# Moving the early samples' sum and its dots behind the last group's matmuls in TensorE's program of a three-layer CIN kernel

## The reference

```python
for (W, b), split in zip(conv_params, split_flags):        # 3 layers
    z = jnp.einsum('bhd,bmd->bhmd', x, x0).reshape(B, h * x0.shape[1], D)
    xk = jax.nn.relu(jnp.einsum('oc,bcd->bod', W, z) + b[None, :, None])
    if split:
        x, xk = (xk[:, :half], xk[:, half:])
    results.append(xk)
pooled = jnp.sum(jnp.concatenate(results, axis=1), axis=2)  # [512, 256]
return pooled @ Wo.T + bo                                   # [512, 1]
```

## Time and profile before

| | before |
|---|---|
| median of 3 runs | 482.07 us (482.01 to 482.96) |
| the profiled execution | 480.3 us |
| its span, first to last instruction | 478.5 us |
| PE busy | 443.9 us (93%) |
| DVE busy | 424.8 us (89%) |
| POOL busy | 408.4 us (85%) |
| ACT busy | 310.7 us (65%) |
| TensorE clock granted, mean | 0.982 |

### The profile page before, as it was taken

One profiled execution on the slowest core, in us unless ns is written; L12 is line 12 of the kernel. 1 busy time (PEld: TensorE's weight loads), 2 busy tenths in 40 slices (PEclk: granted clock), 3 DMA queues, 4 the chain that ended last, 5 costly groups with the idle time before them and its releaser, 6 DMA issues.

```text
span 478.5 us, 5975 instructions
## 1 busy us (share of the span) xinstructions
PE 443.9 (93%) x1601; PEld 302.7 (63%) x1601; DVE 424.8 (89%) x489; ACT 310.7 (65%) x383; POOL 408.4 (85%) x147
## 2 busy tenths in 40 slices
PE   0758599999999999999999999999999999999994
PEld 0325276766667676666767676666767676677672
DVE  1556599999999999999999999999999999999994
ACT  1224667686858677676858677676857677686650
POOL 0107499998999999999999999999999999999991
PEclk9998599999999999999999999999999999999999
DMA  8999999989695959689695959689594954630100
GB/s 210 244 232 223 256 226 209 210 191 205 137 227 120 219 126 221 136 186 209 136 231 112 223 124 222 136 191 204 136 232 112 222 122 98 133 79 10 44 0 1
DMA packets 23232, 78.42 MB, mean 164 GB/s; under 512 B 5939, under 2 KB 5939, under 8 KB 18996
## 3 DMA queue, kind: packets, MB, share of 16 engines
q1 hardware_dynamic: 23220, 78.28, 74.5%
HBM read 61.48 MB, written 0.00 MB: 128 GB/s over the span
## 4 chain that ended last, share of the span: by engine, by line
PE 81%; DMA 6%; DVE 5%; issue 2%; ACT 2%; SPq 2%; POOL 1%; DVEq 0%
PE y_ps L706 25%; PE y_ps L694 14%; PE y_ps L712 14%; PE y_ps L696 14%; PE y_ps L702 7%; DVE z L534 4%; PE y_ps L718 3%; DMA a_rep<-x_sb 3%; DMA w_raw<-w_dram 2%; DMA shifted<-xt_dram 1%; ACT zh L423 1%; PE y_ps L672 1%; POOL zl L481 1%; SPq L329 1%; PE y_ps L698 1%
## 5 line engine op out<-in xcount | busy, mean ns | idle before, releaser
L481 POOL TENSOR_TENSOR zl<-z,zh 128x1024 fp32r<-128x1024 f32 (+1 forms) x141 | 406.6, 2919 | 48.6 <-ACT zh L423 48.2
L534 DVE TENSOR_TENSOR z<-a_ps,b_fac 128x1536 f32<-128x1536 f32 x254 | 269.6, 1083 | 25.7 <-PE y_ps L718 13.2
L423 ACT ACTIVATE zh<-z 128x1024 fp32r<-128x1024 f32 (+1 forms) x141 | 176.8, 1254 | 113.2 <-DVE z L534 112.9
L712 PE MATMUL y_ps<-zl,w_high 128*128 128x512 f32 x332 | 154.6, 559 | 1.9 <-POOL zl L481 1.9
L694 PE MATMUL y_ps<-zh,w_high 128*128 128x512 f32 x332 | 131.9, 397 | 10.1 <-ACT zh L423 10.1
L696 PE MATMUL y_ps<-zh,w_low 128*128 128x512 f32 x332 | 130.8, 394 | 0.0
L706 PE MATMUL y_ps<-z,w_raw 128*128 128x512 f32 x254 | 129.5, 591 | 0.0
L712 PEld LDWEIGHTS y_ps<-zl,w_high 128*128 128x128 f32 x332 | 62.4, 189 | 70.1 <-issue 61.8
L694 PEld LDWEIGHTS y_ps<-zh,w_high 128*128 128x128 f32 x332 | 62.8, 189 | 25.4 <-issue 6.4
L696 PEld LDWEIGHTS y_ps<-zh,w_low 128*128 128x128 f32 x332 | 63.0, 190 | 13.8
L706 PEld LDWEIGHTS y_ps<-z,w_raw 128*128 128x128 f32 x254 | 47.9, 189 | 10.6
(11 more groups left out here) (45 smaller groups left out, 164.8 us busy)
## 6 DMA issues: line engine op xcount, KB each, us to landing
b_fac<-xt_dram SPq DMA_DIRECT2D x60, 512.0 KB, 9.0
shifted<-xt_dram SPq DMA_DIRECT2D x64, 256.0 KB, 4.9
a_rep<-x_sb SPq DMA_DIRECT2D x96, 128.0 KB, 3.0
shifted<-xt_dram SPq DMA_DIRECT2D x64, 128.0 KB, 5.2
a_rep<-x_sb SPq DMA_DIRECT2D x64, 64.0 KB, 2.7
b_fac<-xt_dram SPq DMA_DIRECT2D x8, 256.0 KB, 10.7
w_raw<-w_dram SPq DMA_DIRECT2D x2, 640.0 KB, 13.1
w_raw<-w_dram SPq DMA_DIRECT2D x2, 384.0 KB, 12.5
```

The source lines that it names most:

```text
L423: nc.scalar.activation(zh[:, slot, 0:end - native, :], z[:, slot, native:end, :], ACT.Copy).then_inc(zh_ready, 1)
L481: nc.gpsimd.tensor_tensor(zl[:, slot, 0:end - native, :], z[:, slot, native:end, :], zh[:, slot, 0:end - native, :].bitcast(F32), ALU.subtract
L534: return nc.vector.tensor_tensor(dst, factor.unsqueeze(1).to_broadcast(list(dst.shape)), others, ALU.mult)
L712: mm = nc.tensor.matmul(y, wh[layer][:, w, :], zl[:, slot, t, :], start=False, stop=end_here)
```

## The change

On PE, the sum of the early samples (line 645) and the dots of layers 1 and 2, with their waits, leave the place ahead of the last group and stand behind that group; the order among them becomes dot of layer 1, the sum, dot of layer 2, then as before the dot of layer 3 behind its wait for the last pooling. On DVE, the bias addition over 480 samples leaves the end of `early_samples` and stands behind the last pooling, ahead of the addition for the last 32 samples. No instruction is added, removed or resized.

```diff
@@ early_samples (DVE)
-                dve.wait_ge(out_summed, 1)
-                dve.wait_ge(bo_loaded, 16)
-                nc.vector.tensor_scalar(out_sb[:, 0:EARLY], y_ps[1][0:1, 0:EARLY], bo_sb[0:1, 0:1], None, ALU.add
-                                        ).then_inc(out_ready, 1)
@@ DVE, end of the program
             iterate(dve, body, NCHUNK + 2)
+            dve.wait_ge(out_summed, 1)
+            dve.wait_ge(bo_loaded, 16)
+            nc.vector.tensor_scalar(out_sb[:, 0:EARLY], y_ps[1][0:1, 0:EARLY], bo_sb[0:1, 0:1], None, ALU.add
+                                    ).then_inc(out_ready, 1)
             dve.wait_ge(out_summed, 2)
@@ PE, body
-                    if i_is(i, NCHUNK + 1) and g == GROUPS[3] - 1:
-
-                        pe.wait_ge(ones_set, 1)
-                        pe.wait_ge(terms_made, 3)
-                        nc.tensor.matmul(y_ps[1][0:1, 0:EARLY], ones[:], terms[:], start=True, stop=True
-                                         ).then_inc(out_summed, 1)
-
-                        pe.wait_ge(pooled12_done, NCHUNK + 1)
-                        pe.wait_ge(results_ready[3], NCHUNK - 1)
-                        dot(3, RESULTS[1], pooled12, EARLY, start=True).then_inc(last_begun, 1)
-                        pe.wait_ge(last_begun, 1)
-                        dot(3, RESULTS[2], pooled12, EARLY + SAMPLES)
@@ PE, end of the program
             iterate(pe, body, NCHUNK + 1)
 
+            pe.wait_ge(pooled12_done, NCHUNK + 1)
+            pe.wait_ge(results_ready[3], NCHUNK - 1)
+            dot(3, RESULTS[1], pooled12, EARLY, start=True).then_inc(last_begun, 1)
+            pe.wait_ge(ones_set, 1)
+            pe.wait_ge(terms_made, 3)
+            nc.tensor.matmul(y_ps[1][0:1, 0:EARLY], ones[:], terms[:], start=True, stop=True).then_inc(out_summed, 1)
+            pe.wait_ge(last_begun, 1)
+            dot(3, RESULTS[2], pooled12, EARLY + SAMPLES)
             pe.wait_ge(pooled3_done, NCHUNK)
             dot(4, RESULTS[3], pooled3, EARLY, stop=True).then_inc(out_summed, 1)
```

## The result

| | before | after |
|---|---|---|
| median | 482.26 us (482.01 to 482.96, 4 runs) | 476.32 us (476.04 to 476.51, 4 runs) |
| profiled execution | 480.3 us | 476.04 us (one of the four) |
| its span | 478.5 us | 474.3 us |
| mean granted clock | 0.982 | 0.984 |

The account below looks back on a forecast made before the run. PE waits 2.90 us in program order for terms of a job not needed yet, ahead of a last group mostly ready. -4.51 + 0.45 = -4.06 us, so 482.07 - 4.06 = 478.0 us, range 476.7 to 479.4.

Parts of the forecast that it names:

- Part 1: PE's last group: starts at 466.99, ends at 470.08, 4.51 us earlier; a late POOL costs 0 to 0.3 us.
- The rival in which the ports' exclusion turned round: DVE's first scalar_tensor_tensor begins before POOL's last subtraction, POOL waits 0.7 to 1.45 us: 479.0 us; chance 0.03.
- my mark of 4.4: Sign in the trace after of being wrong: line 520 longer in sum than 4.4 us.
- the one in which PE's instructions come late: Instruction fetch at PE's program end, hidden today by idling, is exposed: 484.0 us if twice; chance 0.03 of being slower.
- Part 2: Last relu and last pooling: same lengths, 0.70 us each, moved by 4.51 us; pooling done at 471.53.
- Part 3: PE's sum and small dots fit the 1.45 us between group's end and last pooling's end, 0.05 to 0.1 spare.
- The rival of the long tail: PE's tail takes longer, the 480-sample addition starts up to 1 us late: gain 3.1 us, 479.0 us; chance 0.05.
- Part 4: DVE's additions at the end: the last ends 1.00 us behind the pooling instead of 0.55, costing 0.45 us.
- The step from the profile to the median: Whole kernel: 4.06 us taken off median 482.07, its 1.8 us above the profiled execution left untouched: 478.0 us.
- The clock had been among my rivals: No gain: PE at its lower clock, last group and tail take twice as long: 482 us; chance 0.03.

Follow-up runs that it names:

- VectorE's part alone: Against the kernel before, the 480-sample addition moved behind the last pooling, TensorE's program unchanged: 482.12 us, ratio 1.0005.
- the second further execution: The kernel before, unchanged, profiled once more to catch an execution in the upper part of its range: 483.48 us.
- the first: The kernel before, unchanged, an earlier extra profiled execution with the same aim: 483.06 us.
- the stall alone: The kernel after, with the wait for terms put back ahead of the last group but no jobs there: 481.22 us.
- the first one: The kernel before, unchanged, its original profiled execution: 480.3 us.
- before again: The kernel before, unchanged, run again: 482.67 us (12 runs); its profiled execution 481.02 us.
- Filling the stall: The kernel before, with twelve matmuls of no use put on TensorE ahead of its wait for terms: 481.24 us, ratio 0.9982.
- the longer stall: The kernel before, with six more VectorE instructions of 128x480 between the two scalar_tensor_tensor instructions, so that terms come later: 485.41 us.

## Why the prediction was right and wrong

**Part 1, the last group: right.** It starts 0.23 us behind the third group and ends at 470.11 (forecast 470.08, with a mark that lies 0.03 later): 4.51 us earlier than before by the common mark. Of this 4.40 is the earlier start (2.90 of idling, the rest the sum and the dots that stood ahead) and 0.11 the quicker run of the group. POOL was done at 468.73 and the load came at 468.83, where the flow has it; whether the native tile would have covered a later POOL no run shows. The rival in which the ports' exclusion turned round didn't occur (POOL's subtraction still leads; line 520 takes 4.49 us for both, 4.45 before, so my mark of 4.4 as a sign of being wrong was set below what before itself shows). Nor did the one in which PE's instructions come late: there is no gap ahead of the group or of the sum.

**Part 2, relu and pooling: right**, both moved along with unchanged length.

**Part 3, the sum and the dots between group and pooling: right.** They run from 470.04 to 471.30 and the pooling's dot starts at 471.61, so the room was 0.3 us. The granted clock is 1.00 from 466 us to the last addition. The rival of the long tail is out.

**Part 4, VectorE's order: right in kind, too dear by half.** The pooling's end to the last addition's end is 0.77 us (471.56 to 472.33), where I had 1.00, so it costs 0.22 us and not 0.45. I had laid the instructions' recorded durations end to end; back to back they start 0.60 and 0.63 us apart though their records say 0.69 and 0.70 (470.87, 471.47, 472.10 above). VectorE's part alone shows the same 0.77. That makes the tail's 4.29 us out of the forecast 4.06.

**The step from the profile to the median: wrong.** I wrote that the median lies 1.8 us above the profiled execution and that nothing in the change touches that difference. That sentence failed. The profiled execution, at 480.3, was near the best that before does (480.2 to 484.3 over all batches), and most of the difference was a price of the very stall that the change removes: 1.62 and 2.77 us in two profiled executions of before. In numbers, the median after is 1.7 us under my 478.0: the surplus of 1.65 and the 0.23 of part 4, less 0.2 by which before's median moved up with its fourth run. The clock had been among my rivals, on the wrong side: I asked whether after could lose it, and took the 1.00 in 467 to 470 us as proof that before kept it. One execution can't show that. In the stretches above the granted clock fell to 0.50 while TensorE idled (the second further execution: 0.98 in the mean from 466 to 470 us, 0.50 from there) or inside the group (the first, 472 to 474 us). The Trainium skill, page TensorE: Matmul & The Clock Gate, section "HAM oscillation — how this bites in real kernels", says that a wait of TensorE for data can throttle it again, so that the next work starts at the lower clock. The second further execution and the stall alone agree, with 2.77 and 2.8 us lost beside a wait of 2.9 and 2.8. The first differs: its work started at full clock and lost it within the group (1.62 us). Three profiled executions with the same wait (the first one, before again and VectorE's part alone) kept 1.00 throughout.

**How much of the surplus is shown.** The medians differ by 5.94 us (4 and 4 runs) and 6.26 (23 and 7), the tails at full clock by 4.29, which leaves 1.65 to 1.97. Filling the stall gave back 1.27 us by the medians (0.1 to 1.6 by the ratio's interval) and 1.85 by the spans, and the four profiles of before carry 1.1 us in the mean. So most of the surplus is shown to be the clock, and by the spans all of it may be; some tenths may be start-up, whose share was not settled. Nor does any run say what decides in an execution when the clock falls.

## What to carry to other kernels

A wait in a TensorE program for an operand that a later job needs, ahead of work that is ready, should be moved behind that work: here it cost its own length, and in about half of the executions up to as much again, because the work behind it ran at 1.2 GHz. Before a saving is scaled from one profile to a median, put the profiled execution among the times: if it stands at their low end, look for what the longer ones have that the profile doesn't, above all an idle stretch of TensorE just ahead of work on the path. Such a stretch can be tried out by filling it with matmuls of no use; if the kernel gets faster and the trace keeps the full clock, the clock was the price. Compare the spans too, since the time around them can change.

## What was not expected of the hardware

- The same program, at the same place, kept its clock through a 2.9 us idle stretch in two profiled executions and lost it in two others, for 1.62 and 2.77 us; with VectorE's part alone it was kept, with the stall alone lost.
- With 5.8 us of idling all four executions lay within 0.9 us, where 2.9 us of idling gave a spread of 3 to 4 us: the longer stall's price looks the more regular, as far as four executions can say, and in its profile it was 2.4 us.
- Twelve useless matmuls made the kernel faster by 1.3 us in the median (ratio 0.9982, interval 0.9966 to 0.9998), and its span by 1.85.
- Six VectorE tensor_scalar instructions of 128x480 took 2.99 us, 0.5 each, with POOL idle; one of the same kind and size (line 515) took 0.84 us with POOL at work beside it. No run separates POOL from other differences between the two.
